# The first norm's weight at its factor, the mask first, unread products in TensorE's waits, and no splits in the last macro tile

## What is computed

```python
def _L0_cond_ref(hidden_states, conditions, ...):
    w_down = down_project[None] * dg[:, None, :] + db[:, None, :]
    act = relu(einsum('bsd,bdh->bsh', hidden_states, w_down))
    w_up = up_project[None] * ug[:, None, :] + ub[:, None, :]
    return einsum('bsh,bhd->bsd', act, w_up) + hidden_states
def _L0_ffn_ref(x, ...):
    h = attn_norm_w * (x * rsqrt(mean(x * x) + EPS))
    qkv = h @ qkv_w + qkv_b            # 16 query heads, 4 key heads, 64 wide
    q, k = _apply_rope(q), _apply_rope(k)
    logits = where(mask, -inf, q k / 8)  # causal within 64 tokens
    attn = exp(logits - logaddexp(lse, attn_sink))
    x = x + (attn v @ proj_w + proj_b)
    h2 = _rmsnorm(x, ffn_norm_w)
    topv, topi = top_k(h2 @ gate_w + gate_b, 4); gw = softmax(topv)
    # every expert: acc + ce * (silu(g) * u @ wd), ce its column of gw
    return x + y2
x + _L0_ffn_ref(_L0_cond_ref(x, cond, ...), ...)
```

## Time and profile before

| | us |
|---|---|
| median of 3 runs | 1204.33 (1200.06 to 1207.04) |
| the profiled execution's own time | 1195.1 |
| its span, first to last instruction | 1193.3 |
| the start and macro tile 0's period, to `project` of tile 4 | 0 to 157.5 |
| five periods after that, `project` of tile 4m to that of tile 4m + 4, each | 66.7 to 68.5 |
| the sixth, to `project` of tile 28 | 496.5 to 563.1 |
| last part of part one, to the start of `begun` | 563.1 to 634.5 |
| experts and final sum | 634.5 to 1193.3 |
| busy: TensorE, VectorE, GpSimd, ScalarE | 988.5, 766.5, 711.0, 451.5 |

### The profile page before, as it was taken

The page is one execution under the profiler, slowest core; times in us unless marked ns, Lnnn a source line. Parts: engine busy times, 40 slices in busy tenths (PEclk is TensorE's granted clock), DMA queues, the critical chain, the costliest instruction groups (busy, mean ns, idle before and its releaser), DMA issues.

```text
span 1193.3 us, 19476 instructions
## 1 busy us (share of the span) xinstructions
PE 988.5 (83%) x6158; PEld 782.7 (66%) x6158; DVE 766.5 (64%) x1702; ACT 451.5 (38%) x1120; POOL 711.0 (60%) x672
## 2 busy tenths in 40 slices
PE   3779799999999998998834888888888888888896
PEld 1557576776767676676723776767767766676675
DVE  3868487776867777784672555555556555555568
ACT  1133243434343353424412444443444444444441
POOL 3426346858586776767485666666666666666550
PEclk8879899999999999998966999999999999999998
DMA  6328976565657756557566755574555546553498
GB/s 177 83 65 272 315 257 197 199 187 198 182 166 238 205 192 202 172 178 209 195 211 212 248 200 202 177 256 158 197 197 192 193 169 231 182 186 129 110 365 315
DMA packets 110749, 239.22 MB, mean 200 GB/s; under 512 B 19171, under 2 KB 48248, under 8 KB 109915
## 3 DMA queue, kind: packets, MB, share of 16 engines
q1 hardware_dynamic: 84042, 192.03, 48.5%
q0 software_dynamic: 19552, 40.02, 10.8%
q10 hardware_dynamic: 7056, 5.91, 1.6%
HBM read 140.37 MB, written 90.05 MB: 193 GB/s over the span
## 4 chain that ended last, share of the span: by engine, by line
PE 56%; DVE 19%; issue 9%; another core or an unknown queue 5%; ACT 4%; POOL 4%; DMA 2%; SPq 0%; ACTq 0%; DVEq 0%; POOLq 0%
PE gbank L984 16%; PE gbank L853 10%; PE gbank L1004 7%; PE gbank L778 4%; DVE ring L1339 4%; PE scores L814 4%; POOL lists L655 3%; ACT in_part L1194 2%; DVE in_part L1572 2%; PE gbank L756 2%; PE scores L995 2%; PE scores L957 2%; PE gbank L827 2%; PE gbank L748 1%
## 5 line engine op out<-in xcount | busy, mean ns | idle before, releaser
L984 PE MATMUL gbank<-ring,in_part 128*128 x954 | 271.4, 421 | 56.4 <-DVE in_part L1572 41.7
L700 POOL DMA_INDIRECT pick_rows<-rows_out,pair_row x156 | 161.0, 1032 | 150.9 <-ACT rows_out L1210 109.1
L984 PEld LDWEIGHTS gbank<-ring,in_part 128*128 128x128 f32 x954 | 173.3, 194 | 97.4 <-issue 67.8
L693 POOL DMA_INDIRECT rows_in<-x_rows,token_row x156 | 152.1, 975 | 55.4 <-issue 40.4
L1572 DVE SCALAR_TENSOR_TENSOR in_part<-scores,norm_w,in_part 128x128 fp32r<-128x128 f32 x318 | 96.3, 345 | 136.7 <-ACT in_part L1194 114.8
L1004 PE MATMUL gbank<-ring,mid_part 128*128 x954 | 155.7, 300 | 12.8 <-DVE mid_part L1593 9.3
L662 POOL TENSOR_TENSOR ring<-ring 128x512 fp32r<-128x512 f32 x96 | 121.0, 1279 | 72.1 <-ACT ring L1149 71.5
L655 POOL DMA_INDIRECT lists<-entry,slot_i x128 | 124.9, 976 | 38.8 <-issue 34.0
L853 PE MATMUL gbank<-w_o,ring 128*128 128x256 f32 x512 | 128.9, 409 | 17.1 <-DVE ring L1322 12.8
L1004 PEld LDWEIGHTS gbank<-ring,mid_part 128*128 128x128 f32 x954 | 126.6, 193 | 20.0 <-issue 19.9
L1210 ACT ACTIVATE rows_out<-gbank,gates 128x256 f32<-128x256 f32 x156 | 74.6, 478 | 154.5 <-PE gbank L1004 97.5
(11 more groups left out here) (169 smaller groups left out, 1495.3 us busy)
## 6 DMA issues: line engine op xcount, KB each, us to landing
w_parts<-ring SPq DMA_DIRECT2D x192, 256.0 KB
ring<-w_parts SPq DMA_DIRECT2D x32, 1536.0 KB
ring<-in_W_up SPq DMA_DIRECT2D x64, 256.0 KB
q_r<-rot SPq DMA_DIRECT2D x32, 512.0 KB, 6.1
picks<-pick_rows SPq DMA_DIRECT2D x8, 2048.0 KB
lists<-in_fill_slots SPq DMA_DIRECT2D x36, 256.0 KB, 5.0
ring<-in_W_down SPq DMA_DIRECT2D x32, 256.0 KB
x_t<-in_x_t SPq DMA_DIRECT2D x8, 512.0 KB, 5.0
```

Of the source, the lines that this page charges most:

```text
L693: e.indirect_dma_start(out=rows_in[i % NG][:, :], out_offset=None, in_=x2_rows, in_offset=bass.IndirectOffsetOnAxis(ap=begun[:, i, 3:4].bi ...
L700: e.indirect_dma_start(out=pick_rows, out_offset=bass.IndirectOffsetOnAxis(ap=begun_row[:, i:i + 1] if i < AHEAD else pair_row[:, i:i + 1] ...
L984: ins = e.matmul(bank[:, :], in_parts[i % 2][x][:, c, :], ring[:, bass.ds(at + y * WE + c * 2 * DFF, 2 * DFF)], start=k == 0, stop=k == le ...
```

## The change

The first norm's weight is no longer multiplied into the product's weights; `apply` multiplies by it together with the factor. The mask and sinks have their own loads and are made before anything else on VectorE; the rest of `constants` becomes `gate`, behind the first `value`. VectorE makes the whole x0 of macro tile 0, and GpSimd's `up(0)` does nothing. A new step `busy` has TensorE multiply ones by ones into the scores' bank, which nobody reads, 18, 9, 12 and 12 times. The lists are reordered; a period has 14 splits, the end none. Not shown: renamed semaphores, the dispatch of the new steps, the rest of SP's list.

```diff
     "PE": ("""
-        down cond up sums pair pair pair pair pair down value score up
+        busy cond down busy up busy sums busy pair pair pair pair pair down value score up
     """, """
-        value score turn_prob score sums attend route_turn project route_turn pair pair turn_prob score
-        route_turn route_turn attend route_pick value pair route_count project pair turn_prob pair
+        value score turn_prob score sums attend route_turn project route_turn pair pair turn_prob
+        route_turn score route_turn attend route_pick value pair route_count project pair turn_prob pair
         attend value value project turn_prob down attend score up project
...
     "DVE": ("""
-        cond down up weights apply pair pair pair pair pair constants down value softmax_a softmax_b up
+        mask cond down up weights apply pair pair pair pair pair down value gate softmax_a softmax_b up
...
         softmax_a value softmax_b apply project softmax_a pair pair softmax_b route_pick value
-        route_count pair project route_list pair softmax_a pair value softmax_b project value down
-        softmax_a up project softmax_b
+        route_count route_list pair project pair softmax_a pair value softmax_b project value down
+        softmax_a up softmax_b project
...
     "ACT": ("""
-        down up weights sums apply down softmax_a up
+        down weights up sums apply down softmax_a up
     """, """
-        turn_prob softmax_a sums attend root apply split route_turn split project route_turn split
-        softmax_a turn_prob route_turn route_turn attend route_pick split turn_prob split project split
-        attend softmax_a split turn_prob split project split down attend split softmax_a up split split
-        project
+        softmax_a turn_prob sums attend route_turn split root apply split project softmax_a route_turn
+        split turn_prob split route_turn split route_turn attend route_pick split turn_prob split
+        project split attend softmax_a split turn_prob split project split down attend split softmax_a
+        up split split project
     """, """
-        turn_prob softmax_a root attend route_turn split split split project route_turn turn_prob
-        route_turn softmax_a split route_turn attend route_pick split project split root turn_prob
-        attend softmax_a split route_turn route_turn split project turn_prob root attend split
-        route_pick split split project split route_turn root route_turn route_pick route_pick
+        turn_prob softmax_a root attend route_turn project route_turn turn_prob route_turn softmax_a
+        route_turn attend route_pick project root turn_prob softmax_a route_turn attend route_turn
+        project turn_prob root attend route_pick project route_turn root route_turn route_pick
+        route_pick
...
     "POOL": ("""
         up pair pair pair pair pair up
     """, """
-        split split pair pair split split pair pair split split pair route_put split split split
-        route_put up route_put split split split route_put
+        split split pair pair split split split split pair pair split split pair route_put split split
+        split route_put up route_put split split split route_put
     """, """
-        split split split split split route_put split split route_put split route_put split split split
-        route_put split route_put route_put route_put route_put
+        route_put route_put route_put route_put route_put route_put route_put route_put
     """),
...
     "SP": ("""
-        load_x_t load_late load_third load_third load_middle load_third load_x_t move move move move
+        load_third load_x_t load_middle load_late load_third load_third load_x_t move move move move
         move
...
         load_x_t fill_lists fill_lists fill_lists store_third load_third fill_lists load_third
-        store_third fill_lists move fill_lists store_third fill_lists load_third fill_lists fill_lists
-        fill_lists fill_lists fill_lists move fill_lists fill_lists load_third fill_lists store_x2
-        fill_lists fill_lists store_third load_third move fill_lists fill_lists store_third store_third
-        fill_lists fill_lists move fill_lists store_x2 move load_third fill_lists fill_lists fill_lists
-        load_third fill_lists store_third fill_lists load_third fill_lists load_third fill_lists
-        store_third store_third fill_lists store_x2 fill_lists store_third fill_lists load_third
+        store_third fill_lists move fill_lists fill_lists load_third load_third fill_lists fill_lists
+        store_third fill_lists fill_lists fill_lists move fill_lists fill_lists load_third store_third
+        fill_lists store_x2 fill_lists load_third fill_lists store_third load_third move store_third
+        fill_lists fill_lists store_third store_third fill_lists fill_lists move fill_lists store_x2
+        move load_third fill_lists fill_lists fill_lists load_third fill_lists store_third fill_lists
+        load_third fill_lists load_third fill_lists store_third store_third fill_lists store_x2
...
+BUSY = (18, 9, 12, 12)
...
+    sinks = [
+        (sink_rows[T:T + SINK_ROWS, :], d["sink"]), (sink_part[T:T + SINK_ROWS, :], d["sink_part"]),
+        (causal_f[0:T, :], d["causal"]), (mask_rows_f[:, :], d["mask_rows"]),
+    ]
     late = [
-        (causal_f[0:T, :], d["causal"]), (mask_rows_f[:, :], d["mask_rows"]),
-        (sink_rows[T:T + SINK_ROWS, :], d["sink"]), (sink_part[T:T + SINK_ROWS, :], d["sink_part"]),
...
+        for dst, src in sinks:
+            e.dma_start(dst, src).then_inc(s_sinks, 16)
...
         w = Once(e)
+        e.memset(ones_b[:, :], 1.0).then_inc(s_ones, 1)
+        e.memset(mask[:, :, :, :], 0.0).then_inc(s_blank, 1)
...
         e.memset(ones[:, :], 1.0)
-        e.memset(ones_b[:, :], 1.0)
...
         def up(m):
+
+            if not m:
+                return
...
-                w.wait_ge(s_u_sum, KC * m + c + 1)
+                w.wait_ge(s_u_sum, KC * (m - 1) + c + 1)
...
+        def busy(k):
+            w.wait_ge(s_ones, 1)
+            for _ in range(BUSY[k]):
+                e.matmul(scores[:, 0, :], ones_b[:, :], ones_b[:, :].unsqueeze(1).to_broadcast([P, 512 // P, P]), start=True, stop=True)
...
         def route_pick(r, banks):
             m, lo, hi = ROOTS[r]
             w.wait_ge(s_x2_t, TPM * m + hi)
+            w.wait_ge(s_w_gate, 1)
...
         def weights():
+            w.wait_ge(s_middle, MIDDLE)
             for n, (whole, parts, at) in enumerate(chunks):
-                w.wait_ge(s_scaled, n + 1)
                 e.activation(parts[:, 0, at], whole[:, at], ACT.Copy).then_inc(s_w_upper, 1)
...
+            for c in range(KC if not m else 0):
+                t_mul, t_add = tmp[1][2 * c], tmp[1][2 * c + 1]
+                w.wait_ge(s_u_add, c + 1)
+                total = own.mark(e.tensor_tensor(t_mul[:, :], t_mul[:, :], t_add[:, :], ALU.add))
+                w.wait_ge(s_vector, total)
+                e.tensor_tensor(x0_t[0][:, c, :], t_mul[:, :], x_t[:, c, :], ALU.add).then_inc(s_x0, 1)
+
         def weights():
-            w.wait_ge(s_middle, MIDDLE)
-            for n, (whole, parts, at) in enumerate(chunks):
-                e.tensor_scalar(whole[:, at], whole[:, at], norm1_w[:, n % KC:n % KC + 1], None, ALU.mult).then_inc(s_scaled, 1)
             for n, (whole, parts, at) in enumerate(chunks):
                 w.wait_ge(s_w_upper, n + 1)
                 e.tensor_tensor(parts[:, 1, at], whole[:, at], parts[:, 0, at].bitcast(F32), ALU.subtract).then_inc(
                     s_w_split, 1)
...
-        def constants():
+        def gate():
             w.wait_ge(s_late, LATE)
-            w.wait_ge(s_memset, ONES)
             for c in range(KC):
                 e.tensor_scalar(w_gate[:, c, :], w_gate[:, c, :], norm2_w[:, c:c + 1], None, ALU.mult)
-            e.tensor_copy(earlier[:, :], earlier_f[:, :])
+            e.tensor_copy(earlier[:, :], earlier_f[:, :]).then_inc(s_w_gate, 1)
+
+        def mask_and_sinks():
+            w.wait_ge(s_sinks, SINKS)
+            w.wait_ge(s_blank, 1)
             e.tensor_copy(mask_rows[:, :], mask_rows_f[:, :])
             e.tensor_copy(mask[0:T, :, :, :].rearrange("p g c k -> p (g c) k"),
...
         def norm1_apply(m, banks):
             w.wait_ge(s_rms1, m + 1)
+            w.wait_ge(s_middle, MIDDLE)
             for c in range(KC):
-                e.tensor_tensor(tmp[0][c][:, :], x0_t[m % 2][:, c, :], gbank[banks[0]][:, :], ALU.mult).then_inc(s_normed, 1)
+                e.scalar_tensor_tensor(
+                    out=tmp[0][c][:, :], in0=gbank[banks[0]][:, :], scalar=norm1_w[:, c:c + 1], in1=x0_t[m % 2][:, c, :],
+                    op0=ALU.mult, op1=ALU.mult).then_inc(s_normed, 1)
```

26 lines of the change are left out of this document (15 added, 11 removed).

## The result

The changed kernel took 1226.94 us (median of 4 runs, 1225.92 to 1228.27), the kernel before 1205.59 beside it: a ratio of 1.0186 (1.0151 to 1.0222). It is 21 us slower, where 1179.8 was forecast. Its profiled execution took 1228.27 us, with a span of 1226.5.

The account below looks back on a forecast made before the run. Bounds: an engine-by-engine chain at a low clock at the start, TensorE in the steady tiles, GpSimd in the tail. Gains 10 + 6 + 8.5 = 24.5 us off 1204.3 give 1179.8 us; 8-in-10 range 1169 to 1191.

Parts of the forecast that it names:

- The start: Up to the first scores: earlier x0, fused weight and TensorE's upper clock level gain 10 us (3 to 12.5).
- Rival 2: Start: the clock isn't up when needed, so the start gives only 3 to 5 us; 1186 us, chance 0.10.
- The order of steps: Steady macro tiles: reordered VectorE and TensorE steps remove waits, gain 1.4 us a tile, 1.0 taken for six periods.
- the 1.16: Steady tiles: TensorE's wait in us for late pairs, before `value`; up to 1.0 us goes, leaving under 0.5.
- the pause before the next `project`: Steady tiles: TensorE's 2.2 us wait for L1322, which waits for the factor; claimed to stay unchanged.
- the two splits more: Each steady period: GpSimd gets 2.5 us more work, other engines have room; cost 0 to 0.7 us a tile.
- Rival 5: Steady tiles: ScalarE's split ahead of `root` and `apply` waits for a late load, making the kernel slower; chance 0.02.
- the tail's: Last stage: without splits GpSimd's 32 stores run back to back and end sooner; gain 8.5 us (7 to 12).
- rival 4: Last stage: something other than GpSimd ends last, so the tail gives only 3 us; 1185 us, chance 0.04.
- The last period keeps its 12 splits and all loads, so its stalls stay: Sixth period, before the last stage: its work is kept, so its stalls were claimed unchanged; no gain or loss priced.

Follow-up runs that it names:

- e1_start: Changed kernel with all five engines' lists for periods and end as before, so only the new start remains; 0.9915 times the kernel before.
- e3_order: Changed kernel with the lists of before for ScalarE, GpSimd and SP (12 splits a period); new start and TensorE/VectorE order stay; 0.9947 times the kernel before.
- e4_move: Changed kernel with SP issuing each period's last copy of rotated queries ahead of two stores of split weights; 1.0244 times the kernel before.
- f_move: e4_move again, beside the changed kernel on one chip; 1.0253 times the kernel before, against the changed kernel's 1.0225.
- c_after: Control: changed kernel with one more register operation per tile of part two, on a faster chip; 1.0048 times the kernel before.
- f_ set: Runs on one slower chip: kernel before (1206.4 us), changed kernel (1.0225), changed kernel with unread GpSimd subtractions between its last stores (1.0142), f_move (1.0253).

## Why the prediction was wrong

**Where the sum went.** Part one was forecast 24.5 us shorter and was 22.6 longer. The start has 11.1 of gain for the 10 forecast, periods 0 to 5 lost 22.7 where 6 were to be won, and the sixth period and the last stage lost 11.0 where 8.5 were to be won.

**The start was right.** x at 9.53 (9.6 forecast), `down` done at 11.6 (11.3), `up` from 14.4 (14.1), x0 complete at 21.84 (21.5), the first pair at 27.47 (27.5), the scores at 51.90 (52). TensorE ran at the upper level from `down` on. Worked out 11.5, taken 10, measured 11.3, and e1_start shows that it lasts. Its first product took 2.00 us where I had 1.7. Rival 2 didn't happen; the clock fell only in the pause of 7.3 us before the scores, as it had in the kernel before.

**The order of steps was over-priced.** I had 1.0 us a tile net of the splits. The waits went in part as said: two of 0.50 and 0.40 us are gone, but the 1.16, which I had put under 0.5, is 0.74, and a new one of 0.39 us stands at 156.76. But e3_order against e1_start makes it 0.1 us a period, in profiles. Two terms are missing in my sum, both read from the profiles and not tested. `route_turn` ahead of `score` made `attend` start 0.6 us later in the period (14.31 against 13.70 behind its first `project`). And the pause before the next `project`, which I let stand at 2.2, grew from 2.40 to 2.81.

```profile
213.95 1.32 PE L869 MATMUL gbank<-w_o,ring 128*128 128x256 f32 x5 [2.40 <-DVE ring L1349]
```
```profile
212.38 1.32 PE L869 MATMUL gbank<-w_o,ring 128*128 128x256 f32 x5 [2.81 <-DVE ring L1349]
```

(e1_start above, e3_order below.) It waits for `apply`, which waits for the sums' factor. The factor came 3.3 us after the sums' start, 2.9 before, for a reason that the trace doesn't show.

**The step that failed** is the one on the two splits more: "ScalarE, SP and the DMA engines have room too (ScalarE is busy 26.8 us of 68, the DMA share is 0.63)". A mean over 68 us. Where the additional stores were put, behind the third move, the share was 0.94 already (e3_order, 182 to 192 us), and 0.03 from 202 to 207; the rest of the traffic went in behind the first move, at 0.60. Worth +13 us in periods 1 to 5 and some 10 in period 0, where the step priced 0 to 0.7 a tile. I had also asked which queue each split was moved past on ScalarE, but not on SP, where the last move of each period now stood behind three stores, all ready. Their order on SP alone isn't the cause: e4_move and f_move took them out of the move's way and were no faster. The clock took its part: of the 5.2 us that period 1 was longer, 3.3 came from products at the lower level behind the new pause of 3.50 us. The pauses of 2.01 and 1.63 us in the same place of the next two periods were followed by the upper level (2.00 and 2.84), one of 3.06 by the lower (4.24 for `up`).

**Rival 5 (slower than before, chance 0.02) had the outcome and the kind of mechanism, but not the place.** A transfer made late by denser traffic holds ScalarE's split, and TensorE behind it. But at the split ahead of `root` and `apply` the load was late by only 1.6 to 1.8 us, and TensorE lost 0.4 us to it at most: the 0 to 0.7 I had priced there held. The waits came at other splits, in period 0 at those ahead of `attend`, for a store, and in e4_move and f_move at the one ahead of `up`'s activation, for a load (2.7 to 4.7 us in every period). The evidence against the rival was the mean share again.

**The second step that failed** is the tail's: "Without the splits the stores end at 584.65 + 40.5 = 625.1" took stores back to back to cost nothing but their own time. Forecast: 71.4 - 8.5 = 62.9 us for the last stage. c_after took 62.1, so the sum was right where nothing stalls. On this case's chip and the f_ set's it took 75.7 and 74.2: the splits between the stores did a second service that I hadn't seen. My rival 4 named "a stall of the attention" with a chance of 0.04 and 3 us left to win, but no mechanism for it; 4.3 us were lost. The rows of before didn't show it: "alternates indirect stores with splits until 633.3" is misread, for the last sixteen stores, from 613.3 on, run unbroken in the kernel before, but by then the last list was all but ready. "The last period keeps its 12 splits and all loads, so its stalls stay" failed too: they stand in other places, and the sixth period took 6.7 us more.

**The range** went wrong by the correlation of the cases: all bounds rested on the same claim of room, so they fell together.

## What to carry to other kernels

Before adding side work "because there is room", take the busy share of the DMA engines in windows of 5 to 10 us, not over a period, and list for each issue what stands behind it on SP and which engine's in-order list waits for its landing. Here six copies in the quiet stretch behind the last stores were free in the periods, and the same six ahead of the last move, half of them at a share of 0.94, cost 2.5 us a period. Time taken out ahead of a wait that another engine ends is not won by that alone: look at what ends the wait. And look what long runs of one kind of instruction a deletion leaves behind.

## What the runs showed of the hardware

- **Indirect stores back to back.** In the three sets of runs on chips of the slower kind, 16 of GpSimd's indirect stores in a row (1.27 us each) kept ScalarE and TensorE waiting 7.8 to 10.5 us for signals long due, in all five profiles; one operation of 1.05 us behind each four took the wait away. A run of eight, one split of 1.3 us and four more came with a like wait (8.5 to 8.9 us on ScalarE) in the sixth period, which was not tested. On the faster kind one kernel with such runs was profiled (c_after), without a wait. By which path GpSimd holds the others up wasn't measured.
- **Chips differ by 9%.** The kernel before took 1205.6, 1191.7, 1098.8, 1206.4 and 1097.1 us in the five sets. The record numbers the chips of the last four 13, 11, 13 and 15, so one chip gave 1191.7 and 1206.4. Part one hardly differs where nothing stalls; part two, with GpSimd's gathers and scatters throughout, takes 558 to 574 us on the one kind and 464 to 470 on the other, and there the waits for "another core or an unknown queue" (5 to 8% of the chain) are absent. That it is the same effect as in the last stage is likely, and was not shown.
- **SP's issues.** The issue directly behind a move of rotated queries took 1.6 to 2.1 us in the median of each of eight profiles, before's among them, where the others took 0.45, and all behind it on SP came later by that. In period 1 of the changed kernel two stores behind the third move took 2.06 and 2.61 us.
